# A six-layer windowed-attention stack on one core: the centring of the second norm as two fp32r products, with the engines' orders of pieces written anew

## The reference, cut to what matters

```
x = attn_layer(shift_tokens(x), ...) + x      # 16 heads of 64, window 32 with the window before it
x = ffn_layer(shift_tokens(x), ...) + x

def ffn_layer(x, g, bln, W1, b1, W2, b2):
    mu = x.mean(-1, keepdims=True)
    var = ((x - mu) ** 2).mean(-1, keepdims=True)
    xn = (x - mu) / jnp.sqrt(var + 1e-05) * g + bln
    hg = xn @ W1 + b1
    a, gate = jnp.split(hg, 2, -1)
    return a * gelu(gate) @ W2 + b2
```

## Time and profile before

| | us |
|---|---|
| runs before | 3597.26, 3596.34, 3588.68 (median 3596.34) |
| the profiled execution, own time | 3587.5 |
| its span in the trace | 3585.7 |
| TensorE (PE) busy | 3356.6 (94%) |
| GpSimd (POOL) busy | 2825.6 (79%) |
| VectorE (DVE) busy | 2802.9 (78%) |
| ScalarE (ACT) busy | 2542.3 (71%) |

### The profile page before, as it was taken

One profiled execution on the slowest core, in us unless ns is written; L12 is line 12 of the kernel. 1 busy time (PEld: TensorE's weight loads), 2 busy tenths in 40 slices (PEclk: granted clock), 3 DMA queues, 4 the chain that ended last, 5 costly groups with the idle time before them and its releaser, 6 DMA issues.

```text
span 3585.7 us, 148597 instructions
## 1 busy us (share of the span) xinstructions
PE 3356.6 (94%) x64228; PEld 2680.1 (75%) x64228; DVE 2802.9 (78%) x4876; ACT 2542.3 (71%) x4686; POOL 2825.6 (79%) x3470
## 2 busy tenths in 40 slices
PE   3798996899999999999999999999999999999997
PEld 2565553778888888888888888887887887888875
DVE  3376665788888888888888888888888888888873
ACT  3333223678888788888887888887888887887863
POOL 1355645889898888898898888888888888888871
PEclk8798998999999999999999999999999999999998
DMA  3332211211121111122111121112111112111110
GB/s 99 97 104 78 86 54 47 54 42 43 44 54 45 47 43 43 43 53 51 39 43 47 49 54 39 43 44 51 46 47 42 41 45 50 42 43 48 38 43 24
DMA packets 126732, 183.45 MB, mean 51 GB/s; under 512 B 29824, under 2 KB 61440, under 8 KB 126080
## 3 DMA queue, kind: packets, MB, share of 16 engines
q1 hardware_dynamic: 119232, 146.15, 16.3%
q0 software_dynamic: 6848, 27.80, 2.6%
HBM read 59.01 MB, written 14.16 MB: 20 GB/s over the span
## 4 chain that ended last, share of the span: by engine, by line
PE 82%; POOL 6%; issue 4%; DVE 3%; ACT 2%; DMA 1%; another core or an unknown queue 0%; POOLq 0%; ACTq 0%; DVEq 0%
PE bank L548 21%; PE bank L611 10%; PE bank L622 9%; PE bank L584 7%; PE bank L558 5%; PE bank L568 4%; PE bank L595 4%; PE bank L685 4%; PE bank L663 3%; PE bank L674 3%; PE bank L463 1%; PE bank L523 1%; PE bank L631 1%; PE bank L502 1%; PE bank L528 1%
## 5 line engine op out<-in xcount | busy, mean ns | idle before, releaser
L548 PE MATMUL bank<-wqkv,xs 128*128 128x512 f32 x3456 | 1045.6, 420 | 21.6 <-DVE m L1059 13.7
L1806 POOL TENSOR_TENSOR m<-m 128x512 f32<-128x512 f32 x576 | 754.6, 1319 | 27.9 <-DVE m L1059 27.7
L548 PEld LDWEIGHTS bank<-wqkv,xs 128*128 128x128 f32 x3456 | 591.8, 191 | 114.4 <-issue 16.7
L1070 DVE TENSOR_REDUCE ss<-sq 128x8 f32<-128x512 f32 x768 | 506.4, 671 | 98.2 <-ACT sq L1418 97.9
L1059 DVE TENSOR_TENSOR m<-bank,tab 128x512 f32<-128x512 f32 x768 | 522.7, 681 | 2.4 <-POOL m L1806 2.4
L1418 ACT ACTIVATE sq<-bank 128x512 f32<-128x512 f32 x768 | 454.7, 599 | 70.1 <-PE bank L548 51.8
L1814 POOL TENSOR_TENSOR S<-S,nw 128x1024 f32<-128x1024 f32 x192 | 367.0, 1911 | 106.7 <-DVE S L1090 102.1
L611 PEld LDWEIGHTS bank<-P,big 64*64 64x64 f32 x24576 | 379.6, 135 | 95.5 <-issue 94.3
L1057 DVE TENSOR_TENSOR m<-bank,tab 128x512 f32<-128x512 f32 x576 | 392.5, 681 | 44.9 <-PE bank L568 19.2
L1822 POOL TENSOR_TENSOR S<-S,rs 128x512 f32<-128x512 f32 x384 | 396.9, 1050 | 30.4 <-DVE rs L1104 29.8
L611 PE MATMUL bank<-P,big 64*64 64x32 f32 x24576 | 402.8, 220 | 7.8 <-issue 7.6
(11 more groups left out here) (229 smaller groups left out, 6572.2 us busy)
## 6 DMA issues: line engine op xcount, KB each, us to landing
big<-vst SPq DMA_DIRECT2D x1536, 64.0 KB, 2.0
stage<-in_wqkv SPq DMA_DIRECT2D x36, 256.0 KB, 3.1
tab<-in_tab SPq DMA_DIRECT2D x48, 128.0 KB, 2.2
xsort<-big SPq DMA_DIRECT2D x4, 960.0 KB, 8.4
big<-xsort SPq DMA_DIRECT2D x12, 256.0 KB, 7.4
ysort<-big SPq DMA_DIRECT2D x12, 256.0 KB
wo<-in_wo SPq DMA_DIRECT2D x6, 512.0 KB, 3.6
big<-in_x SPq DMA_DIRECT2D x8, 256.0 KB, 3.5
```

The costliest lines, as they stand in the source:

```text
L548: m = eng.matmul(pb[:, :], xt[a], wqkv[:, z, 512 * part:512 * part + 512], start=(n == 0), stop=(n == 2))
L1070: eng.tensor_reduce(ss[:, g // 2 % 2, a:a + 8], sq[:, part % 2, :].rearrange("p (h d) -> p h d", d=DH), axis=X_AX, op=ALU.add).then_inc(s[ ...
L1806: eng.tensor_tensor(turned(g, part), turned(g, part), m2[:, part % 2, :], ALU.add).then_inc(s["g_add"], 1)
```

## The change

What it does:

- `centre` becomes two fp32r products, `center` by the high half of x2s and `center` by its low half, summed in PSUM. `center` is now a tensor of its own in fp32r; its two values (1 - 1/128 and -1/128) are exact in it. The other norms still use it as fp32 through a bitcast.
- The halves of x2s go into the slot (u + 1) % 2 of `xs`, which stands idle between the last projection of unit u + 1 and the refill for unit u + 3. ScalarE's `shifted` gets one more Copy of 128 by 512, which waits until those projections are done. VectorE gets the new piece `x2_low`, a subtraction of 128 by 512.
- Because that slot is used, `high` and `low` of the next unit must wait for `centre` (`p_lnc`), and ScalarE runs `high(u + 1)` where it ran `high(u + 2)`, directly ahead of `centred`; VectorE's `low` moves behind `rotate(91, 1)` in the stretch shown below.
- In the preamble the matrix `center` is loaded by a DMA of its own into `x2s`, and ScalarE's first instruction copies it into `center`. The semaphore `d_ws` is dropped: the first weights count on `d_x0`.
- The lists of pieces are written anew on all four engines.

```diff
+        center = sb("center", [P, P], F32R)
...
-            eng.dma_start(kc[:, :], kc_d).then_inc(s["d_kc"], 16)
+            eng.dma_start(kc[:, :], kc_d[:, 0:KC_N - P]).then_inc(s["d_kc"], 16)
+            eng.dma_start(x2s[:, 0:P], kc_d[:, KC["center"]]).then_inc(s["d_kc"], 16)
...
             def centre(u):
-                pe.wait_ge("a_x2s", 3 * u + 3)
+                pe.wait_ge("v_x2s", u + 1)
                 pb = claim(norm_home("centre", u))
-                eng.matmul(pb[:, :], kc[:, KC["center"]], x2s[:, :], start=True, stop=True).then_inc(s["p_lnc"], 1)
+                eng.matmul(pb[:, :], center[:, :], xs[:, (u + 1) % 2, 0, :], start=True, stop=False)
+                eng.matmul(pb[:, :], center[:, :], xs[:, (u + 1) % 2, 1, :], start=False, stop=True).then_inc(s["p_lnc"], 1)
...
             def low(u):
                 dv.wait_ge("a_hi", u + 1)
+                if u > 2:
+                    dv.wait_ge("p_lnc", u - 2)
...
+            def x2_low(u):
+                dv.wait_ge("a_x2s", 4 * u + 5)
+                eng.tensor_tensor(xs[:, (u + 1) % 2, 1, :], x2s[:, :], xs[:, (u + 1) % 2, 0, :], ALU.subtract).then_inc(s["v_x2s"], 1)
...
-            ac.wait_ge("d_kc", 32)
+            ac.wait_ge("d_kc", 48)
+            eng.activation(center[:, :], x2s[:, 0:P], ACT.Copy, scale=1.0, bias=0.0).then_inc(s["a_x2s"], 1)
...
             def shifted(u):
-                ac.wait_ge("a_x2s", 3 * u + 3)
+                ac.wait_ge("a_x2s", 4 * u + 4)
+                ac.wait_ge("p_proj", min(24 * (u + 2), 6 * NG))
+                eng.activation(xs[:, (u + 1) % 2, 0, :], x2s[:, :], ACT.Copy, scale=1.0, bias=0.0).then_inc(s["a_x2s"], 1)
```

More of the change, by code:

```diff
@@ L63, in columns @@
     return out, at
-KC, KC_N = columns([("ident", 128), ("center", 128), ("heads", 16), ("mean", 1), ("rank", 8), ("mask", 3 * 64)])
+KC, KC_N = columns([("ident", 128), ("heads", 16), ("mean", 1), ("rank", 8), ("mask", 3 * 64), ("center", 128)])
 WA, WA_N = columns([("ws", 128), ("wg", 128), ("router", 8), ("sg", 256), ("su", 256), ("sd", 256), ("below", 128),
@@ L694, in end_centre @@
                 pb = claim(close_home("centre", u))
-                eng.matmul(pb[:, :], kc[:, KC["center"]], Xr[:, u % NC, :], start=True, stop=True).then_inc(s["p_ec"], 1)
+                eng.matmul(pb[:, :], center[:, :].bitcast(F32), Xr[:, u % NC, :], start=True, stop=True).then_inc(s["p_ec"], 1)
                 vacant[close_home("centre", u)] = [("a_e", 2 * k + 2)]
@@ L722, in _ @@
                 if q4 == 0:
+                    variance(u - 3)
+                    sim(n - 3)
                     end_variance(u - 6)
@@ L727, in _ @@
                     probs(n - 4, 0)
+                    probs(n - 4, 1)
                     proj(n, 1)
-                    probs(n - 4, 1)
                     out_proj(n - 5)
@@ L755, in _ @@
                     proj(n, 5)
+                elif q4 == 2:
                     gate(u - 4, 2)
-                    sim(n - 2)
-                    turn_q(n, 0)
-                    proj(n + 1, 0)
-                    turn_q(n, 1)
-                    probs(n - 3, 0)
-                    proj(n + 1, 1)
-                elif q4 == 2:
+                    sim(n - 3)
+                    turn_q(n - 1, 0)
+                    turn_q(n - 1, 1)
+                    proj(n, 0)
+                    probs(n - 4, 0)
                     probs(n - 4, 1)
+                    proj(n, 1)
                     out_proj(n - 5)
@@ L772, in _ @@
                     spread(u - 3)
-                    turn_k(n - 2, 0)
-                    proj(n, 3)
-                    turn_k(n - 2, 1)
-                    proj(n, 5)
+                else:
+                    turn_k(n - 3, 0)
+                    proj(n - 1, 3)
+                    turn_k(n - 3, 1)
+                    proj(n - 1, 5)
                     end_spread(u - 6)
-                    sim(n - 2)
-                else:
+                    sim(n - 3)
                     turn_q(n - 1, 0)
@@ L796, in _ @@
                     proj(n, 5)
-                    variance(u - 2)
-                    sim(n - 2)
             for par in range(2):
@@ L801, in _ @@
                 vacant[6 + par] = [("a_oev", 2 * NG)]
+            gate(NU - 4, 2)
+            sim(NG - 1)
+            probs(NG - 2, 0)
             end_spread(NU - 6)
@@ L1193, in _ @@
                     reduced(n - 1, 1)
+                    rotate(n - 1, 1)
+                    weights(n - 1, 1)
+                    low(u)
                     rotate(n - 1, 2)
@@ L1270, in _ @@
             hidden(NU - 4, 1)
+            x2_low(NU - 2)
             end_step(NU - 5)
@@ L1287, in _ @@
             end_step(NU - 4)
+            x2_low(NU - 1)
             norm_step(NU - 1)
@@ L1562, in _ @@
             high(0)
-            high(1)
             for n in range(NG + 2):
@@ L1590, in _ @@
                     square(n, 0)
-                    square(n, 1)
                     exps(n - 3)
                     gelu(u - 4, 0)
+                    square(n, 1)
                     gelu(u - 4, 1)
@@ L1599, in _ @@
                     masked(n - 2)
+                    square(n, 3)
+                    v_out(n, 1)
+                    gelu(u - 4, 2)
                 elif q4 == 2:
-                    square(n - 1, 3)
-                    v_out(n - 1, 1)
-                    gelu(u - 4, 2)
                     out_turned(n - 5, 0)
@@ L1643, in _ @@
                     square(n, 3)
+                    out_turned(n - 4, 0)
                     weights(n, 2)
                     v_out(n, 1)
-                    high(u + 2)
+                    weights(n, 3)
+                    xn_high(u - 3)
                     turned_q(n, 0)
+                    turned_q(n, 1)
                     out_turned(n - 4, 1)
@@ L1835, in _ @@
                 if q4 == 0:
-                    divide(n - 4, 0)
+                    add(n - 1, 1)
                     divide(n - 4, 1)
@@ L1843, in _ @@
                     scale(n - 2, 1)
-                    add(n, 0)
-                    add(n, 1)
                 elif q4 == 1:
+                    add(n - 1, 0)
+                    add(n - 1, 1)
                     divide(n - 4, 0)
@@ L1853, in _ @@
                     add(n - 1, 3)
-                elif q4 == 2:
-                    scale(n - 3, 1)
-                    add(n - 1, 0)
-                    add(n - 1, 1)
-                    divide(n - 4, 0)
-                    add(n - 1, 2)
+                    scale(n - 2, 1)
+                    add(n, 0)
+                    add(n, 1)
+                    add(n, 2)
+                    divide(n - 3, 0)
+                elif q4 == 2:
                     divide(n - 4, 1)
```

146 lines of the change are left out of this document (70 added, 76 removed).

## The result

The changed kernel takes 3604.49 us (median of 9 runs, 3600.66 to 3608.32); the kernel before, run beside it, 3593.22 us (median of 9, 3588.68 to 3599.70). The ratio is 1.003, with an interval of 1.002 to 1.004: **slower by 0.3%, 11 us**. The forecast was 17 us faster, and its range ended at 3597. The profiled execution took 3604.49 us, with a span of 3602.7.

A forecast was written before the change was run, and what follows sets the result against it. TensorE was taken as the bound. Product -17.9, `turn_k` +1.7, start -1.3 and tail +0.5 sum to -17.0 us, set against a median of 3596.34: 3579.3 us, range 3567 to 3597.

The forecast's parts named there:

- The product: `centre` on TensorE falls from 0.86 to 0.47 us, saving 0.39 us in each of 46 units, 17.9 us less.
- the first of the four on what covers the added work: `x2_low` on VectorE, even at 1.84 us, ends over 1 us ahead of `centre`, so it costs nothing there.
- `x2_low`: Added VectorE subtraction, expected to behave as `low`: 0.68 us at least, 0.81 at the median, 1.84 at most.
- The second rival: VectorE and GpSimd hold each other up; TensorE waits 1.0 us a unit; 28 us slower, 3624 us; chance 0.10.
- rival 1: Long subtractions make TensorE wait 0.2 us ahead of `turn_k` in most units: 9 us given back, 3587 us; chance 0.17.
- `turn_k`: TensorE waits there for GpSimd's chain: 0.04 us a unit on average, 1.7 us more, bounds 0 to 14 us.
- The start: ScalarE's table loads early, first activation near 6.6 us instead of 7.90, carried through to the end: 1.3 us less.
- The tail: In the last unit's norm a Copy and a subtraction are added, some product time goes: 0.5 us more, between 0 and 1.4.
- The swaps costed at nothing: GpSimd's other pieces swapped in twos and threes, and `probs(g, 1)` 0.7 us earlier on TensorE: no cost.

The follow-up runs named there:

- run 8: Changed kernel with `x2_low` moved early in VectorE's list and `centre` put back to one fp32 product: 3576.37 us, ratio 1.0002 to the kernel before.
- run 1: Changed kernel with `residual` moved up directly behind `x2_low` in VectorE's list: 3577.03 us, ratio 0.9956 to the kernel before.
- run 2: Changed kernel with `x2_low` moved up in VectorE's list, ahead of `summed`: 3569.38 us, ratio 0.9942 to the kernel before.
- run 5: Kernel before with `residual` moved behind `rotate(n, 0)` and `reduced(n, 0)` on VectorE: 3598.61 us, ratio 1.0066 to the kernel before.
- run 6: Kernel before with `residual` moved later on VectorE, behind `rotate(n, 1)` too: 3642.67 us, ratio 1.0185 to the kernel before.
- run 7: Kernel before with an early ScalarE Copy of 128 columns, so the function table loads early: 3574.49 us, ratio 0.9993 to the kernel before.
- run 3: Changed kernel with `centre` as one fp32 product of x2s again, all orders kept: 3612.39 us, ratio 1.0053 to the kernel before.
- run 4: Changed kernel without `x2_low`, both products of `centre` reading the high half: 3568.50 us, ratio 0.9931 to the kernel before.

## Why the prediction was wrong

- **The product** was right: 0.23 us each, 0.38 us a unit by run 8 in place of 0.39, and run 8 puts its whole worth at 18 to 21 us.
- **The step that failed** is the first of the four on what covers the added work. It reads "`x2_low` must be done before `centre`", and asks of it alone whether it ends in time. It does, 2.1 us ahead. What was never listed is the second thing that `centre` waits for, a free bank 3, which `residual` gives; and `residual` was moved behind `x2_low`, a rotation and a sum of squares. The printed order shows this move, and the text took it for a relief ("`residual` no longer stands ahead of the rotation"). In the unit that the forecast followed, `residual` waits for `out_proj` (L622) and ends 2.1 us ahead of the `centre` at 2127.74:

```profile
2125.36 0.29 DVE L1114 TENSOR_TENSOR Xr<-bank,Xr 128x128 f32<-128x128 f32 x1 [0.25 <-PE bank L622]
```

In the unit shown of the changed kernel 4.3 us lie between the end of `lessened` and the start of `residual`: 2.0 for `x2_low`, the rest for a rotation and two sums of squares. That takes all there was to spare, and over 42 units it cost 4.5 us of waits ahead of `centre` and 14.6 in and ahead of `values`, as much as the product saved. Moving one of the two is enough: `residual` alone (run 1) or `x2_low` alone (run 2) gives 1.7 us to spare again.

- **`x2_low`** was taken at 0.7 us, 0.81 at the median of `low`, with 1.84 as the bound; it took 2.02 us in 46 of 48 units, over that bound. The second rival had this mechanism, and of it the half that counts is right: VectorE is held in nearly every unit. The Trainium skill (SBUF — State Buffer, SBUF: two separate sides) says that VectorE's instructions with two SBUF inputs and GpSimd's take turns at a shared pair of ports, each for its whole instruction; the trace agrees: in the unit shown, `x2_low` ends 0.55 us behind `weighed`. But the rival let this delay end at `turn_k`, with 1.0 us a unit and 3624 us. There the trace has 6.3 us in 12 times, and run 1, with as long an `x2_low` and 10.3 us there, is faster than before. The bound of the range goes by the same path: its terms (rival 1 with 14 us ahead of `turn_k`, the highest run as base) add up to about 3592 us and not to 3597, and the measured 3604.49 is over both.
- **`turn_k`**: 1.7 us more forecast, 3.9 more measured in the list of waits; a matter of size.
- **What no step had**: 14.6 us in `values`, and the lower clock of units 0 and 1. I read the 22.4 us that wait for nothing ahead of `sim` as a fixed feature. They could have said that TensorE's stream stops in places, and that elsewhere a lead hides it: the kernel before has 6.9 us of such stops in `values` too. Runs 5 and 6 show what a late release costs there: over the 42 units 7.4 us in and ahead of `values` beside 1.9 at `centre` in run 5, and 17.7 beside 22.0 in run 6.
- **The start**: the first activation came at 6.43 us, where 6.6 was forecast, and the table loaded at 0.72 us. What it waited for last was TensorE's first product (0.98 us), and not the copy of `center`, which the forecast had as the only thing between. That this carries through to the end is not shown: the first `low` of the changed kernel was 3.4 us later than before, and that of run 7 was 4 to 6 us earlier than in runs 5 and 6. **The tail** lost nothing (43.8 us from the last `centre` to the end, 44.4 before), where 0.5 was forecast.
- **The swaps costed at nothing** were, by run 8, nothing, as far as that run can separate them from the added Copy and subtraction.

What stays open: whether the stops of up to 1.8 us in `sim`, 15 to 27 us in every kernel here, could be hidden too by an earlier release ahead of them. They stand at the same step of 256 records. That was not tried.

## What to carry to other kernels

For an instruction that a change makes faster or moves, list every semaphore it waits for, the one for its bank too, and follow each back to where the new order puts its releaser. A release must come well ahead of the waiting engine, not just in time: here 1.65 us was enough, and at 0.66 us TensorE lost time in the short products behind, though hardly any at the wait. And look at the granted clock where a wait grew: in the changed kernel and runs 3, 5 and 6 TensorE waits 2.2 us or more ahead of `centre` in units 0 and 1, and in 7 of these 8 cases the clock fell to its lower level in the wait or within 1.6 us behind it, for 3.4 to 10.2 us. And an added VectorE instruction with two inputs in SBUF is placed by what GpSimd starts just ahead of it: 0.68 us in one place, 2.02 in another.

## What the runs showed that I had not expected

- A stop of up to 1.3 us in a row of products without a wait, at the same product in the same unit of four kernels with different orders on the other engines, all at a step of 256 records, and hidden behind `centre` wherever the last release before it came 1.65 us early (none in runs 1, 2 and 4 and in the kernel before).
- A wait of 2.2 us ahead of `centre` is followed by 6.8 us at the lower clock in units 0 and 1 of the changed kernel; a wait of 0.7 us there in the kernel before is not.
- Delays of a release cost more than they show at the wait: `residual` 1.4 us later cost 24 us in all (run 5), of which 4.1 us are waits of `centre` from 800 us on; one piece more cost 66 us (run 6).
- ScalarE's table load depended on where the first wait stood: behind the first product it ran at 6.60 us, with a Copy ahead that waits for a transfer it ran at 0.72, while the transfer was under way.
